# Weight splits and bias adds on GpSimd moved between the halves of an attention's maxima, and scaling put ahead of a norm, in a two-layer transformer kernel

## What is computed

```python
x = x + attn_a(layernorm(x), Wq, Wc, Wk, Wv, Wo)        # latent K and V, rotary, softmax
x = x + ffn(layernorm(x), lora_A, lora_B, W, bias, lora_weights)
x = x + attn_b(layernorm(x), w_attn, b_attn, w_proj, b_proj)  # ALiBi, causal softmax
x = x + ffn(layernorm(x), lora_A, lora_B, W, bias, lora_weights)
```

## Time and profile before

| | |
|---|---|
| median of 3 runs | 1751.6 us (1749.39 to 1755.77) |
| the profiled execution | 1751.5 us, span 1749.3 us |
| PE busy | 1636.4 us, 94% of the span |
| DVE busy | 1407.0 us, 80% |
| ACT busy | 967.6 us, 55% |
| POOL busy | 213.9 us, 12% |
| attention b | about 1156 to 1630 us of the span |
| last stage | 1633 to 1749 us |

### The profile page before, as it was taken

The page is one execution under the profiler, slowest core; times in us unless marked ns, Lnnn a source line. Parts: engine busy times, 40 slices in busy tenths (PEclk is TensorE's granted clock), DMA queues, the critical chain, the costliest instruction groups (busy, mean ns, idle before and its releaser), DMA issues. The chain is left out here.

```text
span 1749.3 us, 32974 instructions
## 1 busy us (share of the span) xinstructions
PE 1636.4 (94%) x13040; PEld 840.3 (48%) x13040; DVE 1407.0 (80%) x2959; ACT 967.6 (55%) x1095; POOL 213.9 (12%) x272
## 2 busy tenths in 40 slices
PE   6998999999999999999899999999999999999888
PEld 3554333333333333333345677655455555554667
DVE  3776799999999999999358354668888888899675
ACT  2433278888788887887711112136666666667210
POOL 3332200000000000000032021021111100003331
PEclk9999699999999999999999999989999999999999
DMA  6665434343333333331140443664746453642211
GB/s 216 224 187 188 83 57 82 65 65 65 63 60 72 57 56 57 57 59 60 60 154 25 144 127 120 202 140 63 120 70 97 74 101 70 96 78 88 92 66 72
DMA packets 116801, 167.58 MB, mean 96 GB/s; under 512 B 20772, under 2 KB 58036, under 8 KB 116532
## 3 DMA queue, kind: packets, MB, share of 16 engines
q1 hardware_dynamic: 115176, 160.99, 40.5%
q0 software_dynamic: 1472, 4.49, 1.3%
HBM read 100.41 MB, written 64.50 MB: 94 GB/s over the span
## 5 line engine op out<-in xcount | busy, mean ns | idle before, releaser
L360 DVE TENSOR_REDUCE mxp<-ps_m 128x1 f32<-128x512 f32 x1280 | 802.9, 685 | 53.9 <-PE ps_m L326 48.1
L696 ACT ACTIVATE a_p<-a_ps_s 128x1024 f32<-128x1024 f32 x512 | 524.6, 1025 | 155.8 <-PE a_ps_s L609 146.4
L696 ACT ACTIVATE b_p<-b_ps_s 128x1024 f32<-128x1024 f32 (+1 forms) x320 | 294.7, 938 | 159.4 <-PE b_ps_s L609 155.9
L357 DVE CUSTOM_DVE_ANT_0 ps_m<-ps_m,b_masks 128x128 f32<-128x128 f32 (+3 forms) x512 | 240.1, 517 | 44.3 <-PE ps_m L326 39.4
L326 PE MATMUL ps_m<-slot_qk 62*128 62x512 f32 (+3 forms) x624 | 229.7, 451 | 11.9 <-DVE mxp L360 9.0
L326 PE MATMUL ps_m<-a_slot_qk 62*128 62x512 f32 x640 | 236.0, 449 | 0.9 <-DVE mxp L360 0.9
L609 PE MATMUL a_ps_s<-a_slot_qk 64*128 64x512 f32 x640 | 235.2, 445 | 0.0
L633 PE MATMUL a_ps_o<-a_p,a_slot_v 128*32 128x256 f32 x2560 | 207.7, 391 | 8.8 <-ACT second_v L687 8.7
L609 PEld LDWEIGHTS a_ps_s<-a_slot_qk 64*128 64x128 f32 x640 | 95.6, 185 | 131.7 <-issue 130.9
L283 POOL CAST cparts<-negm 128x16 fp32r<-128x16 f32 x64 | 12.6, 197 | 1108.3 <-DVE negm L366 1108.3
L609 PE MATMUL a_ps_s<-slot_qk 64*128 64x512 f32 x384 | 137.9, 457 | 0.0
(11 more groups left out here) (217 smaller groups left out, 2421.3 us busy)
## 6 DMA issues: line engine op xcount, KB each, us to landing
va_tokens<-w_o SPq DMA_DIRECT2D x16, 512.0 KB, 3.2
ka_parts<-pa_parts SPq DMA_DIRECT2D x16, 512.0 KB, 3.0
qa_parts<-pa_parts SPq DMA_DIRECT2D x32, 256.0 KB, 3.7
kb_parts<-slot_memory SPq DMA_DIRECT2D x16, 512.0 KB, 3.5
qb_parts<-slot_memory SPq DMA_DIRECT2D x32, 256.0 KB, 3.4
vb_tokens<-w_proj SPq DMA_DIRECT2D x16, 512.0 KB, 2.7
a_slot_qk<-qa_parts SPq DMA_DIRECT2D x60, 128.0 KB, 4.1
a_slot_qk<-ka_parts SPq DMA_DIRECT2D x48, 128.0 KB, 6.4
```

Source lines behind the costliest of these rows:

```text
L357: dve.tensor_tensor_reduce(from_, from_, mask_of_query[:, CHUNK - keys:], 1.0, LOWEST, ALU.add, ALU.max, accum_out=to).then_inc(piece_take ...
L360: dve.tensor_reduce(to, from_, AX.X, ALU.max).then_inc(piece_taken, 1)
L696: act.activation(p_sb[:, (2 * u + pair) % NP, :, off:CHUNK], ps_s[:, 2 * pair:2 * pair + 2, off:CHUNK], ACT.Exp, scale=scale).then_inc(exp ...
```

## The change

In attention b POOL's side work now stands between the two halves of a group's maxima, in a function `between_maxima(g)`. The load of `w_proj` follows the first-half maxima of group 2. The cut of `w_proj` follows those of group 4, that of `w_eff` those of group 5. The 16 bias adds follow those of groups 6 to 9, four at a time. In the last stage the DVE's scaling and low parts of chunk k+1 stand ahead of the norm of chunk k.

```diff
-                adds = iter(to_add)
-                for g in range(1, NG):
-                    for qh in range(2):
-                        parts_of_maxima(g, qh)
-                        for tile, bias in itertools.islice(adds, 1):
-                            pool.tensor_tensor(tile, tile, bias, ALU.add)
+                def between_maxima(g):
                     if g == 2:
                         for to, source in late:
                             pool.dma_start(to, source).then_inc(late_loaded, 16)
+                    n = g - 4
+                    if 0 <= n < len(to_split):
+                        whole, high, low_part = to_split[n]
+                        pool.wait_ge(late_loaded, 16 * len(late))
+                        pool.tensor_copy(high[:, :, :], whole[:, :, :]).then_inc(w_high_ready, 1)
+                        pool.wait_ge(w_high_ready, n + 1)
+                        pool.tensor_tensor(low_part[:, :, :], whole[:, :, :], high[:, :, :].bitcast(F32),
+                                           ALU.subtract).then_inc(w_split, 1)
+                    n = 4 * (g - 4 - len(to_split))
+                    if 0 <= n < len(to_add):
+                        for tile, bias in to_add[n:n + 4]:
+                            pool.tensor_tensor(tile, tile, bias, ALU.add)
+
+                for g in range(1, NG):
+                    parts_of_maxima(g, 0)
+                    between_maxima(g)
+                    parts_of_maxima(g, 1)
                 pool.wait_ge(late_loaded, 16 * len(late))
-                for n, (whole, high, low_part) in enumerate(to_split):
-                    pool.tensor_copy(high[:, :, :], whole[:, :, :]).then_inc(w_high_ready, 1)
-                    pool.wait_ge(w_high_ready, n + 1)
-                    pool.tensor_tensor(low_part[:, :, :], whole[:, :, :], high[:, :, :].bitcast(F32),
-                                       ALU.subtract).then_inc(w_split, 1)
...
+                if fast and 2 <= k + 1 < NC:
+                    output.scale(dve, k + 1)
+                    output.low(dve, k + 1)
                 if k < NC:
                     f_norm.vector(dve, k, k, k and (lambda: banks.wait_full(dve, f_turns[k - 1][-1])))
-                if 2 <= k + 1 < NC:
+                if not fast and 2 <= k + 1 < NC:
                     output.scale(dve, k + 1)
-                    if fast:
-                        output.low(dve, k + 1)
```

More of the change, by code:

```diff
@@ L1 @@
 from contextlib import ExitStack
-import itertools
 import numpy as np
```

## The result

The changed kernel takes 1731.7 us (median of 4, 1726.4 to 1734.8) where the kernel before took 1750.5 on the same chips (median of 4): a ratio of 0.9893, 95% interval 0.9875 to 0.9912, some 19 us. The forecast was 1733.2 us in a range of 1728 to 1738.

What follows compares the result with a forecast made beforehand. The prediction took PE, busy 94% of the span, as the bound, with idle gaps at the seam and in the last stage. Gains of 15.1 + 1.8 + 1.5 = 18.4 us gave 1733.2 us, range 1728 to 1738.

Steps and rivals of the forecast that it cites:

- Part 1: Last stage: scaling and low parts ahead of the norm close two PE gaps and the low clock behind; gain 15.1 us.
- The slacks: Last stage: low parts, norm and residual (f,0) are ready before PE needs them, each with 2 to 5 us to spare.
- the gaps: Last stage: PE idles twice, losing 4.97 us each; slow products at low clock behind add 2.74 and 2.38 us.
- Part 2: Seam between second attention and last stage: splits leave POOL's end, PE restarts 3.55 us earlier; gain 1.8 us after clock terms.
- the first seam: Seam of the first attention: PE idles 3.54 us and its clock is low until 6 us after restart; same expected here.
- The low clock behind the new restart: Seam: clock taken as low from 1629.9 to 1636.4, costing 3.25 us, against 1.5 in the kernel before.
- Rival (a): Seam: the clock does not fall there, so the seam gives 5.05 us and the kernel takes 1730.0 us; chance 0.15.
- Part 3: Inside the attention: splits and bias adds on POOL do not hold the DVE's masked maxima; cost 0.
- (d): Attention: the splits alone hold the DVE's maxima for 14 us, PE behind; up to 1747 us; chance 0.05.
- (e): Attention: POOL's successive operations hold the DVE whatever it reads, 34 us from splits and adds; slower, 1767 us; chance 0.03.
- Part 4: Group 2: w_proj load issued after first-half maxima removes PE's wait on shift rows; gain 1.5 us; w_o's move taken as 0.
- The sum: Whole kernel: 15.1 + 1.8 + 1.5 = 18.4 us gained, giving 1733.2 us; chance 0.62.

Runs made afterwards that it cites:

- e1: The kernel before with only the last stage's new order (scaling and low parts ahead of the norm): 1735.9 us against 1751.3, ratio 0.9913.
- e2: The changed kernel with the last stage back in its old order, so only POOL's part is changed: 1744.7 us against 1751.3, ratio 0.9962.
- e5: The changed kernel plus 14 unread products on PE filling its idle time at the seam: 1733.9 us, ratio 0.9877 to the kernel before.
- e8: The changed kernel plus three unread DVE products of two SBUF operands, two beside POOL's split operations, one with POOL idle: 1743.9 us.

## Why the prediction was right

**Part 1** said 15.1 us and is 15.1 (103.4 to 88.3), in e1 too. Its steps came out one by one: scaling 2.5 us without POOL's adds beside it, the norm ended at 1671.6 where PE's transposes came at 1677.1, and the residual of (f,0) was over at 1674.0. The slacks were 5.2, 5.5 and 3.1 us, where 2 to 5 were expected. The load was not late. What made this sum right is that a third of the price of the gaps was read beyond them, in the products at low clock behind. That it fits to 0.1 us is luck of the comparison: against the old order in e2 (102.0) the same part is worth 13.6 us, since that third varies from trace to trace.

**Part 2** said 1.8 us. Against the trace of before it is 2.3, against the two other traces with the old seam 3.5 to 3.9. The mechanism was right in each link: the scalings at 2.48 us (3.3 assumed), the reciprocals issued right behind the load, the DVE done at 1625.9, and the seam hanging on SP's last stores (PE 0.44 us behind them, 0.3 assumed). The clock fell again, as the first seam had suggested. Two terms were mis-sized. The low clock behind the new restart was put at 6.5 us (cost 3.25) and lasted 5.5 (1630.9 to 1636.4, cost 2.6 in the products of chunk 0); that its end at 1636.4 agrees with the prediction's is chance, as the whole seam lies about 1 us later in this trace. And the seam of before was a short one: one trace gave 6.98 us of idle, two more gave 8.09. Rival (a) was not what happened; e5 shows it would have been worth 2.4 us.

**Part 3** said nothing, and nothing it is: 452 ns, and groups as long as before. Rivals (d) and (e) fell. e8 and the residuals of the last stage show that their mechanism exists and that the operands decide.

**Part 4** said 1.5 us and is 1.6 between the two traces, 1.0 to 1.6 over all. The K and Q loads beside it cost nothing that shows, and neither does the load of w_o in attention a: from group 2's first-half maxima to group 3's there it is 41.7 us before and 41.6 after, and 41.6 to 41.7 in the eleven other traces, with the load in either place.

**The sum** of 18.4 stands against 19.0 from the stretches (15.1 + 2.3 + 1.6) and 19 to 20 us from the ratios of the two comparisons. That it comes so close is partly luck: by the other traces with the old order or the old seam part 1 is up to 1.5 us smaller and part 2 up to 1.6 larger. So is the time of the profiled run (1734.8 against 1733.2): 2.2 us of chance at the start and 4.9 lost near group 15 stand behind it. The prediction held no term for a fall of the clock inside an attention.

## What to carry to other kernels

Where one engine serves another in a fixed order, put first what the other asks for first, and read the price of a gap of PE up to the last product at low clock, not to the restart, in more than one trace. Side work for GpSimd was free here beside VectorE operations that read at most one operand from SBUF (452 ns with and without it); one that reads two waited for the rest of GpSimd's instruction, 3.76 us for a work of 0.28. So cut or place GpSimd's long operations by what VectorE runs at that time. Compare two traces by stretches between fixed events: here the new last stage was 88.3 to 88.4 us in all eleven traces that have it, while whole runs of the changed kernel differed by 8.

## What the runs showed of the hardware that was not expected

A wait of PE of only 0.95 us inside a busy attention can be followed by 10 to 14 us at the half clock (12 us at 0.50 above), which cost 3.6 to 4.9 us; it came in six of nine traces with the wait. Behind a longer wait the time at half clock differs from trace to trace as well: 3.0 to 6.1 us after the seam's restart, 3.7 and 5.7 us behind the same gap of 4.80 us in e2 and before. At the seam 14 idle-time products kept the clock at 2.4 GHz, for 2.4 us of gain against the two traces of the changed kernel. And an operation of the DVE of 0.28 us took 3.76 us beside one of POOL, ending 0.15 us after it.
